# A six-layer decoder step on one core: constants by ScalarE, products of ones in TensorE's first waits, a causal mask by GpSimd, and the orders around them

## What is computed

```python
x = x + L0_attn(ln(x))     # 16 heads of 16, rotary, causal softmax, exact fp32 weights
x = x + L0_xattn(ln(x))    # fp8-rounded activations and 256x256 matrices
x = x + L0_ffn(ln(x))      # 16 experts of 176, top 4 in 2 of 4 groups, and shared experts
x = x + L1_attn(ln(x))     # as L0_attn, int8 activations, ternary weights
x = x + L1_xattn(ln(x))    # four experts of 256, chosen by the token's number
x = x + L1_ffn(ln(x))      # gated 1024-wide layer, ternary weights, an RMS norm inside
```

```python
scores = einsum('bhqd,bhkd->bhqk', q, k) / sqrt(16)
scores = where(tril(ones(S, S)), scores, -inf)
attn = softmax(scores, axis=-1)
op = einsum('bhqk,bhkd->bhqd', attn, v)
```

## Time and profile before

| what | us |
|---|---|
| median of 3 runs | 560.38 |
| profiled execution | 562.76 |
| its span | 561.0 |
| TensorE busy | 515.5 |
| VectorE busy | 423.1 |
| ScalarE busy | 309.2 |
| GpSimd busy | 156.8 |
| first gate starts at | 126.35 |
| first hash gate starts at | 434.14 |

### The profile page before, as it was taken

How to read it: one execution, slowest core, us unless ns; L and a number is a source line. 1 busy time by engine, 2 the same in 40 slices (tenths; PEclk the granted TensorE clock), 3 DMA queues, 4 the chain that set the end, 5 groups by cost and what they waited for, 6 DMA issues and landing times.

```text
span 561.0 us, 11757 instructions
## 1 busy us (share of the span) xinstructions
PE 515.5 (92%) x4741; PEld 361.6 (64%) x4741; DVE 423.1 (75%) x981; ACT 309.2 (55%) x532; POOL 156.8 (28%) x202
## 2 busy tenths in 40 slices
PE   1479997979999999999999999999999999989965
PEld 0144543536777887777877786767777677667644
DVE  3868897788867878567787768665684578799994
ACT  2155854645674245673286672477434762845596
POOL 3708385830010016200001704001320010133362
PEclk9999998969999999999999999999999999999999
DMA  8044052220000002000000201000000300000001
GB/s 258 2 176 140 39 177 89 87 77 1 1 1 2 2 1 76 3 1 1 1 2 1 76 1 46 33 1 2 1 2 1 113 1 1 2 2 1 2 21 53
DMA packets 5841, 21.04 MB, mean 38 GB/s; under 512 B 891, under 2 KB 3067, under 8 KB 5020
## 3 DMA queue, kind: packets, MB, share of 16 engines
q1 hardware_dynamic: 5788, 20.30, 10.7%
HBM read 19.25 MB, written 1.05 MB: 36 GB/s over the span
## 4 chain that ended last, share of the span: by engine, by line
PE 77%; DVE 16%; ACT 4%; issue 2%; DMA 1%; POOL 0%; SPq 0%; ACTq 0%; DVEq 0%
PE ps L982 27%; PE ps L1016 15%; PE ps L738 4%; PE ps L861 3%; PE ps L791 3%; PE ps L722 3%; PE ps L992 3%; PE ps L796 3%; PE ps L834 3%; PE ps L842 3%; PE ps L760 2%; DVE nmx L2363 2%; PE ps L845 2%; PE ps L715 1%; PE ps L880 1%
## 5 line engine op out<-in xcount | busy, mean ns | idle before, releaser
L1818 ACT ACTIVATE hs<-ps 128x512 f32<-128x512 f32 (+1 forms) x68 | 39.4, 583 | 65.4 <-PE ps L982 65.2
L2363 DVE TENSOR_REDUCE nmx<-ps 128x2 f32<-128x512 f32 (+1 forms) x96 | 60.7, 683 | 14.6 <-PE ps L796 14.5
L2468 DVE TENSOR_TENSOR hs<-hs,ps 128x512 f32<-128x512 f32 (+1 forms) x68 | 45.5, 669 | 28.5 <-PE ps L982 22.1
L527 POOL TENSOR_TENSOR ve<-mv,half 128x2 f32<-128x2 f32 x24 | 5.2, 215 | 189.9 <-DVE mv L2257 189.9
L1825 ACT ACTIVATE hh<-hs 128x512 f16<-128x512 f32 (+1 forms) x52 | 31.6, 610 | 42.7 <-PE ps L1016 25.3
L1016 PE MATMUL ps<-w2h,hh 128*128 128x256 f16 x200 | 54.8, 274 | 0.0
L1016 PE MATMUL ps<-w2l,hh 128*128 128x256 f16 x200 | 54.5, 273 | 0.0
L1016 PE MATMUL ps<-w2h,hl 128*128 128x256 f16 x200 | 54.5, 273 | 0.0
L2474 DVE TENSOR_TENSOR hs<-hs,ps 128x512 f32<-128x512 f32 (+1 forms) x52 | 34.6, 665 | 17.2 <-PE ps L992 16.2
L2479 DVE TENSOR_TENSOR hl<-hs,hh 128x512 f16<-128x512 f32 (+1 forms) x52 | 39.9, 773 | 9.0 <-ACT hh L1825 8.8
L1777 ACT ACTIVATE pk<-ps 128x512 f32<-128x512 f32 x64 | 34.5, 598 | 15.1 <-PE ps L845 14.1
(11 more groups left out here) (242 smaller groups left out, 1310.6 us busy)
## 6 DMA issues: line engine op xcount, KB each, us to landing
stage<-in_w SPq DMA_DIRECT2D x12, 800.0 KB, 4.3
tstage<-in_tern SPq DMA_DIRECT2D x4, 1024.0 KB, 4.9
cs<-in_ctxT SPq DMA_DIRECT2D x1, 1024.0 KB, 9.8
cd<-in_ctxT SPq DMA_DIRECT2D x1, 1024.0 KB, 4.8
out_x<-xs SPq DMA_DIRECT2D x4, 256.0 KB, 2.2
w0s<-in_w SPq DMA_DIRECT2D x1, 768.0 KB, 6.7
xs<-in_x SPq DMA_DIRECT2D x1, 768.0 KB, 8.1
lnwb<-in_lnw SPq DMA_DIRECT2D x1, 512.0 KB, 5.6
```

The lines of the kernel that those rows point to most:

```text
L1818: act.activation(hs[:, n % 3, 0:w], ps[:, gate_bank(n), 0:w], ACT.Silu).then_inc(e_sil.sem, 1)
L2363: dve.tensor_reduce(nmx[:, int(n % 3 > 0), first + par:first + 2 * heads:2], ps[:, max_bank(it, n) + par, :].rearrange("p (h k) -> p h k", ...
L2468: TT(hs[:, n % 3, 0:w], hs[:, n % 3, 0:w], ps[:, up_bank(n), 0:w], ALU.mult).then_inc(e_hb.sem, 1)
```

## The change

1. `masks_made` on ScalarE makes `idb`, both masks and `selh` behind `first_weights_high(1)`. VectorE's `constants_made` keeps two small copies and moves to iteration 1.
2. `awake_first` issues products of `ctk`, which is all ones then, as soon as GpSimd has cleared it, ahead of `first_turn(0)` (25), `project(0, 0)` (30) and `project(0, 1)` (22), 256 columns each.
3. In iterations 2 to 6 (the third to the seventh) `scores_exp` has no mask product. GpSimd sets the exponentials above the diagonal to 0 with `affine_select` (`limited`), in place, two instructions a unit, and `values` waits for `pm_ok` in place of `p_ok`.
4. `sels` and `cT` have 128 rows instead of 33 (the added rows of `sels` are zeros).
5. The lists of calls of TensorE, VectorE, ScalarE and GpSimd are written in another order nearly throughout, and TensorE has 147 fillers of 512 columns instead of 129.

```diff
+def is_limited(it):
+    return 2 <= it < 7
...
-    sel0 = np.zeros((33, MOE_PAD), np.float16)
+    sel0 = np.zeros((P, MOE_PAD), np.float16)
...
-        cT = sb("cT", [33, T], F16)
+        cT = sb("cT", [P, T], F16)
...
+            def limited(it, n):
+                for par in range(2):
+                    g.wait_ge(p_ok.sem, p_ok.at(it, 2 * n + par + 1))
+                    part = pk1[n // 3][:, par, :].rearrange("p (h q) -> p h q", q=P) if n % 3 == 0 else \
+                        pk0[:, n % 3 - 1, par, :].rearrange("p (h q) -> p h q", q=S)[:, :, 0:P]
+                    g.affine_select(part, part, [[0, 4 if n % 3 == 0 else 2], [1, P]], ALU.is_ge, 0.0, base=0,
+                                    channel_multiplier=-1).then_inc(pm_ok.sem, 1)
...
+            def awake_first(bank, count):
+                pe.wait_ge(k_pool.sem, 1)
+                for _ in range(count):
+                    pe.matmul(ps[:, bank, 0:2 * P], ctk[:, 0, :], ctk[:, :, :], start=True, stop=True, skip_group_check=True)
...
                 for par in range(2):
+                    if is_limited(it):
+                        break
                     bank = ps[:, first + par, :].rearrange("p (h q) -> p h q", q=width)
                     pe.matmul(bank[:, :, 0:P], idb[:, :], mask_kq[:, 0:len(tiles), :],
...
-                                          start=False, stop=False, skip_group_check=True)
+                                          start=(is_limited(it) and i == 0), stop=False, skip_group_check=True)
...
-                pe.wait_ge(p_ok.sem, p_ok.at(it, 6 * (grp // 2) + 4 + 2 * (grp % 2)))
+                ready = 6 * (grp // 2) + 4 + 2 * (grp % 2)
+                if is_limited(it):
+                    pe.wait_ge(pm_ok.sem, pm_ok.at(it - 2, ready))
+                else:
+                    pe.wait_ge(p_ok.sem, p_ok.at(it, ready))
...
+            awake_first(1, 25)
             first_turn(0)
+            awake_first(1, 30)
             project(0, 0)
+            awake_first(1, 22)
             project(0, 1)
+            awake(1, 22)
             stack(0, 0)
             stack(0, 1)
...
+            def masks_made():
+                act.wait_ge(d_c.sem, 32)
+                act.activation(idb[:, :], ident, ACT.Copy)
+                act.activation(mask_qk[:, :, :], cst[:, None, C_QK:C_QK + P].to_broadcast([P, 4, P]), ACT.Copy)
+                act.activation(mask_kq[:, :, :], cst[:, None, C_KQ:C_KQ + P].to_broadcast([P, 4, P]), ACT.Copy)
+                act.activation(selh[:, :, :], cst[:, C_SELH:C_SELH + H, None].to_broadcast([P, H, P]),
+                               ACT.Copy).then_inc(k_const.sem, 1)
...
             first_weights_high(1)
+            masks_made()
             stacks(0, 0)
```

More of the change, by code:

```diff
@@ L1332, in _ @@
             gate(14)
             up(14)
+            spread(14)
+            down(12)
+            gate(15)
             scores_exp(3, 0)
-            spread(14)
-            gate(15)
             up(15)
@@ L1357, in _ @@
-            down(16)
+            values(3, 1)
             spread(18)
-            up(18)
-            values(3, 1)
-            scores_exp(3, 3)
+            down(14)
+            gate(19)
             up(19)
             stack(4, 0)
+            back(3, 0)
+            down(15)
+            stack(4, 1)
             scores_exp(3, 4)
-            back(3, 0)
-            stack(4, 1)
-            gate(19)
+            gate(20)
+            spread(19)
+            stack(4, 2)
             scores_exp(3, 5)
-            stack(4, 2)
+            down(16)
@@ L1908, in _ @@
             maxima_turned(1)
+            slices(5)
             slices(6)
```

1232 lines of the change are left out of this document (628 added, 604 removed).

## The result

The changed kernel takes 553.48 us (median of 4, 552.79 to 554.18), the kernel before 559.85 us (median of 4) beside it: a ratio of 0.9877, 95% interval 0.9844 to 0.9909: 6.9 us less by the ratio, 6.4 us by the two medians. The forecast was 539.1 us (-21.3 us), with 528 to 554 for its range. The direction was right, a third of the size came. The profiled execution of the changed kernel has a span of 552.0 us at a mean granted clock of 0.981, against 561.0 us at 0.988 before.

The account below looks back on a forecast made before the run. The prediction took TensorE, busy 305.63 of 306 us, to bound the mixed stage and a VectorE-led chain the start. Start -12, masks -10.3, waits +1 and tail 0 gave -21.3 us: 539.1 us, range 528 to 554 us.

Parts of the forecast that it names:

- Start of -12 us at the first gate: Up to the first gate (126.35 us before): new start and reordering bring it 12 us earlier, from -5 to -17.
- The turned maxima: Early chain, iteration 0: the maxima are turned 12.7 us earlier, forecast at 38.5 us against 51.15 before.
- rival (a): Iterations 0 and 1: another late link gives back half the start, -5 us, masks -8.5, +1: 548 us; chance 0.24.
- The products of ones: First waits of TensorE: 77 products raise the clock early, -1.8 us on the first projection, between +2.5 and -2.0 each.
- the +1: Mixed stage (128 to 434 us): all waits behind selects, with GpSimd's blocking of VectorE, cost 1 us, from 0 to +6.
- The selects' length: GpSimd in iterations 2 to 6: 60 selects of 1.0 and 0.5 us take 40 us in all.
- Masks of -10.3 us: Mixed stage: mask products removed from TensorE come off the end, 10.3 us, between 8.5 and 11.5.
- The matrix of 128 rows at nothing: Selection matrix grown from 33 to 128 rows: TensorE streams 256 columns all the same, so no time change.
- the tail at 0: Tail, rewritten with 22 more fillers of 512 columns in waits: 0 us, from -4 to +4.
- (e): Selects or ternary blocks stand before due inverse roots, about 2 us in each of eight places: 554 us; chance 0.05.
- (c): Mixed stage: masks are not on the path, waits refill TensorE's time, only the start counts, -8: 552 us; chance 0.07.
- (d): Mixed stage: selects lock VectorE out until it is the bound, over 106 us of selects; 586 us at 120; chance 0.04.

Follow-up runs that it names:

- before_masks: The kernel before with only the causal masks of iterations 2 to 6 moved to selects on GpSimd, order and start unchanged: 583.52 us, 1.0406 of before.
- before_no_masks: The kernel before with the causal mask of iterations 2 to 6 left out, nothing else changed: 554.72 us, 0.9898 of before.
- before_masks2: The kernel before with the selects on GpSimd and the second ternary block behind the fifth iteration's low parts and selects: 582.34 us, 1.0405 of before.
- the cut kernels: The changed kernel, and mask variants of it, with GpSimd's 2048-element instructions (ternary blocks, context's split) cut into 512-element pieces; with selects kept 0.9698 to 0.9724 of before.
- all_pieces: The changed kernel with GpSimd's 2048-element instructions of the ternary blocks and the context's split cut into pieces of 512: 545.20 us, 0.9724 of before.
- all_pieces_again: The same kernel as all_pieces, measured again: 544.02 us, 0.9698 of before.

## Why the prediction was wrong

- **Start of -12 us at the first gate.** The turned maxima held to 0.2 us, by luck in part: the steps before them were 0.5 to 1 us late, and the maxima of iteration 0 turned at 51.1 us in the profile of before, but at 47.2, 47.9 and 48.2 us in three kernels with the same start (`before_masks`, `before_no_masks`, `before_masks2`). The first gate came 9.9 us earlier by the pair of profiles, 6.6 us by the means of four. What was missing is the context's split, which I had noted as lying "on GpSimd between the slices" and had given no price: it locks VectorE for 3.72 and 4.17 us, TensorE waits 4.7 us, and cutting it is worth 4 to 5.5 us. It is the mechanism of rival (a). The products of ones were priced too low: -1.8 us, and they bring 4.2 us at the maxima and 6.5 by the ratio.
- **GpSimd beside VectorE: the step that failed.** "In the mixed stage VectorE has 306 - 224 = 82 us of slack, so 40 us of blocking, were all of it to hit, would be absorbed in sum; I price it inside the +1." Slack is a sum over the stage. A blocked instruction costs when what TensorE needs next stands behind it, whatever VectorE does later. The selects' length was overestimated (29.8 us, not 40) and their cost underestimated: 4.0 to 5.4 us. The ternary blocks I had not priced at all; I looked for the queue (an inverse root behind a block) and not for what runs beside the block in its new place: 4.5 us. With the split that is 12 to 15 us where the sum has 1, most of the 14.4 us between forecast and result.
- **Masks of -10.3 us: mis-sized.** The sentence "what TensorE no longer has to do there comes off the end" held in the cut kernels, for 8.5 us: the columns, without the change-over. In the kernel before, busy 305.63 of 306 us, the same products brought 7.0 us, since VectorE and ScalarE were only a fraction of a microsecond earlier at many places. A share of 100% says that TensorE is the last to be late, not by how much.
- **The matrix of 128 rows at nothing, and the tail at 0.** "TensorE streams 256 columns all the same, nothing" left out the change of rows, which gained about 4 us. The tail cost: from the first hash gate to the last product it takes 126.0 us, 2.7 us more than before, and 125.8 to 128.0 us in all the other kernels of the new order, against 122.1 to 123.4 us in those of the old. Which of its new fillers and moves does that was not tried.
- **Rivals.** (e) gave 554 us and (c) 552 us, the nearest in number, and neither by its mechanism: in the changed kernel VectorE waits 3.6 us in all for inverse roots (2.1 before), not 2 us in each of eight places, and the masks are on the path. What happened is (a)'s late link at the split, and the lock of (d) at single places instead of over the stage: VectorE is busy 74% of it (228.22 of 308 us). The condition of (d) has a slip: with -12 us at the start the change loses from 82 + 12 us of selects on, not 82 + 24; they took 29.8 us, so nothing hangs on it. I had weighted each rival as if it came alone, when several came at half size.

With the cuts the kernel runs at 0.9698 to 0.9724 of before (intervals 0.9661 to 0.9757), 544 to 545 us, better than both: a good half of the 14.4 us that were missing against the forecast.

## What to carry to other kernels

The work taken off an engine at 100% of a stage bounds the gain; the gain itself is known only once the next engine's lead is read, wait by wait, and a run that leaves the work out measures it cheaply. Count the columns of a removed product and not the change-over before the next one, which stays; and look at where the number of rows changes from product to product. Another engine's slack is no cover for a blocked instruction that stands ahead of what the full engine waits for. When work moves on GpSimd, list what VectorE does beside it at the new place, and keep each GpSimd instruction as short as the shortest VectorE work that others wait for: four of 512 elements in place of one of 2048 gave more here than the change itself. A wait added in an in-order queue is priced by everything behind it: the same selects made the kernel 23 us slower in an order not made for them. Before two single profiles are compared, take out the time at the lower clock.

## What the runs showed that I had not expected

- GpSimd's instructions hold VectorE even for two elements a row: 1.67 us against 0.18 us for the same `sf` with the pieces.
- A pair of 33-row products among 128-row ones costs 0.20 us more than a pair of 128 rows, at the changes of rows, though both kinds show 271 to 273 ns from start to end.
- The clock differs between executions of one program. The same stretch of the cut kernel, first in `all_pieces`, then in `all_pieces_again`:

```profile
112.00:116.00 4.00, 4.00 (x37) 3.22 (x34) 3.52 (x10) 2.19 (x5) 0.00 (x0) 1.00 0.38 160
```

```profile
112.00:116.00 4.00, 3.78 (x19) 2.63 (x19) 3.48 (x6) 0.60 (x1) 0.00 (x0) 0.50 0.23 96
```

One has full clock, the other half, and the first gate is 2.4 us later. In the second TensorE had waited 1.94 us at 107.76 us for `o`; in the first the longest there was 0.62 us:

```profile
107.76 0.39 PE L853 MATMUL ps<-mask_qk,idb 128*128 128x256 bf16 x2 [1.94 <-DVE o L2460]
```

A start term read from one profile carries such a difference with it.
